# A routed two-expert FFN behind a conditional FFN: first eight sequences in pieces of two, first weight loads ahead of their rows, last piece ranked ahead of the tiles

## What is computed

```python
# 1. conditional FFN: one set of 32 output columns depends on the sequence's index
h = gelu(x @ fc1_w.T + fc1_b)                      # (32, 128, 512)
shared = h @ fc2_w.T + fc2_b                       # 96 columns
expert_x = einsum('bnh,bph->bnp', h, experts_w[indices]) + experts_b[indices]   # 32 columns
y = concatenate([shared, expert_x], -1)            # (32, 128, 128)
# 2. mixture of 8 experts, the top 2 of each token
scores = y @ router_w.T                            # (4096, 8)
top_v, top_i = top_k(scores, 2); routing_w = softmax(top_v)
out = sum over e of (gelu(y @ w1[e].T) @ w2[e].T) * (weight of e for the token)
return x + out
```

## Time and profile before

| | us |
|---|---|
| median of 3 runs | 244.78 |
| lowest and highest of the 3 | 243.59, 251.19 |
| the profiled execution's own time | 242.82 |
| its span (first to last instruction) | 241.1 |
| PE busy | 212.0 (88%) |
| POOL busy | 165.4 (69%) |
| DVE busy | 149.9 (62%) |
| ACT busy | 125.8 (52%) |

### The profile page before, as it was taken

The page is one execution under the profiler, slowest core; times in us unless marked ns, Lnnn a source line. Parts: engine busy times, 40 slices in busy tenths (PEclk is TensorE's granted clock), DMA queues, the critical chain, the costliest instruction groups (busy, mean ns, idle before and its releaser), DMA issues.

```text
span 241.1 us, 3554 instructions
## 1 busy us (share of the span) xinstructions
PE 212.0 (88%) x1107; PEld 168.3 (70%) x1107; DVE 149.9 (62%) x458; ACT 125.8 (52%) x178; POOL 165.4 (69%) x172
## 2 busy tenths in 40 slices
PE   7999999999996269989999999999999999998200
PEld 2768678668766248868888888888888888887100
DVE  3454275366756057869999999986666652213593
ACT  2566745744753026856677666666777623241000
POOL 6306527777777777587878778877887777776710
PEclk9999999999999555999999999999999999999955
DMA  6665546563711695099948966666699918414968
GB/s 171 195 208 169 132 160 198 134 197 123 230 59 45 210 372 234 25 367 366 357 165 284 384 254 238 235 224 230 236 329 371 360 58 263 184 50 137 361 228 325
DMA packets 25860, 53.45 MB, mean 222 GB/s; under 512 B 4936, under 2 KB 11344, under 8 KB 23794
## 3 DMA queue, kind: packets, MB, share of 16 engines
q1 hardware_dynamic: 19648, 42.55, 51.6%
q0 software_dynamic: 4544, 8.54, 10.2%
q10 hardware_dynamic: 1650, 2.16, 2.5%
HBM read 24.34 MB, written 13.02 MB: 155 GB/s over the span
## 4 chain that ended last, share of the span: by engine, by line
POOL 44%; issue 23%; PE 13%; DVE 8%; DMA 7%; ACT 2%; SPq 1%; POOLq 0%; ACTq 0%; DVEq 0%
POOL results L442 28%; POOL slots L435 16%; PE hp L852 4%; PE dd L863 3%; DMA w<-ffn 3%; DMA results<-rows,back_row 2%; PE hp L908 2%; DVE z L832 2%; DVE z L830 2%; PE tr L877 1%; DMA slots<-y_rows,slot 1%; DMA cexp_bias<-in_cexp_b 1%; ACT hs_raw L501 1%; PE misc L841 0%; DVE ffn L725 0%
## 5 line engine op out<-in xcount | busy, mean ns | idle before, releaser
L442 POOL DMA_INDIRECT results<-rows,back_row x78 | 93.0, 1193 | 24.8 <-issue 23.5
L435 POOL DMA_INDIRECT slots<-y_rows,slot x64 | 66.6, 1041 | 37.5 <-DVE slot L632 19.2
L908 PE MATMUL hp<-xs,w 128*128 128x512 f32 x192 | 52.7, 413 | 2.1 <-DMA w<-ffn 2.1
L501 ACT ACTIVATE hs_raw<-hp 128x1024 f32<-128x1024 f32 x32 | 32.8, 1026 | 33.2 <-PE hp L908 33.2
L908 PEld LDWEIGHTS hp<-xs,w 128*128 128x128 f32 x192 | 38.2, 200 | 11.2 <-issue 2.5
L739 DVE TENSOR_TENSOR hs<-hs_raw,hs 128x1024 fp32r<-128x1024 f32 x32 | 39.0, 1219 | 2.8 <-ACT hs L509 2.4
L509 ACT ACTIVATE hs<-hs_raw 128x1024 fp32r<-128x1024 f32 x32 | 33.9, 1061 | 0.5
L467 ACT ACTIVATE hs_raw<-hp,fc_bias 128x512 f32<-128x512 f32 (+1 forms) x36 | 22.8, 640 | 20.3 <-PE hp L852 20.3
L863 PE MATMUL dd<-cond,hs_raw 128*128 128x128 f32 x256 | 32.3, 278 | 0.0
L863 PEld LDWEIGHTS dd<-cond,hs_raw 128*128 128x128 f32 x256 | 30.0, 192 | 0.8 <-issue 0.8
L852 PE MATMUL hp<-xs_raw,fc 128*128 128x512 f32 (+1 forms) x72 | 29.6, 555 | 0.0
(11 more groups left out here) (142 smaller groups left out, 263.6 us busy)
## 6 DMA issues: line engine op xcount, KB each, us to landing
w<-ffn SPq DMA_DIRECT2D x16, 1024.0 KB, 5.5
picked<-slots SPq DMA_DIRECT2D x16, 264.0 KB, 2.8
ffn_raw<-in_wT SPq DMA_DIRECT2D x8, 512.0 KB, 4.7
z<-results SPq DMA_DIRECT2D x8, 512.0 KB, 7.2
narrow_w<-in_wT SPq DMA_DIRECT2D x7, 512.0 KB, 7.5
cond<-in_cexpT SPq DMA_DIRECT2D x32, 64.0 KB, 2.0
x_rows<-in_x SPq DMA_DIRECT2D x1, 2048.0 KB, 10.4
out<-z ACTq DMA_DIRECT2D x8, 256.0 KB, 2.9
```

Source lines behind the costliest of these rows:

```text
L435: pool.indirect_dma_start(out=slots, out_offset=bass.IndirectOffsetOnAxis(ap=slot[:, p, n:n + 1], axis=0), in_=y_rows[:, p % YB, k, r, :], ...
L442: pool.indirect_dma_start(out=results, out_offset=bass.IndirectOffsetOnAxis(ap=back_row[:, t, r:r + 1], axis=0), in_=rows[:, t % RB, r, :] ...
L501: act.activation(hs_raw[:, (NP + t) % 2, 1, g, :], hp[:, g, :], ACT.Gelu).then_inc(c_gelu, 1)
L908: mm = pe.matmul(hp[:, g, n * TILE:(n + 1) * TILE], w[:, t % WB, 0, part, f * P:(f + 1) * P], xs[:, (NP + t) % XB, v, :], start=m == 0, st ...
```

## The change

The first eight sequences are cut into four pieces of two in place of two of two and one of four, so there are ten pieces and `LAST` = 9; `LIST_PIECE` still names the pieces that end at the same sequences. The eight experts are loaded in pieces 0 to 5 (`RAW`) and split two at a time in pieces 4 to 7 (`SPLIT`). `spread_bias(0)` moves behind `up(0)`, `spread_bias(1)` behind `down(1, ...)`, and both use other PSUM banks. SP reads the first list and loads the weights of tiles 0 to 2 before it waits for the scatters of their rows. The last piece's `score` and `rank` on PE, `y_second` and `lean` on ACT, and `choose`, `mark` and `place_pairs` on DVE move ahead of most of the work of tiles 0 to 2. `tile_done` leaves ACT: DVE counts tile t - 3 in `rows_of(t)`, which waited for that landing already, and POOL counts the last three, the first of these before the last tile's scatters.

```diff
@@ -35,14 +35,14 @@
...
-PIECES = (2, 2) + (4,) * (CHUNKS - 1)
+PIECES = (2, 2, 2, 2) + (4,) * (CHUNKS - 2)
 NP = len(PIECES)
...
-LIST_PIECE = (5, 7, LAST)
+LIST_PIECE = (LAST - 3, LAST - 1, LAST)
 LIST_WIDE = (3, 4, 9)
@@ -59,6 +59,11 @@
...
+RAW = ((0,), (1,), (2,), (3,), (4, 5), (6, 7)) + ((),) * (NP - 6)
+SPLIT = ((),) * 4 + ((0, 1), (2, 3), (4, 5), (6, 7)) + ((),) * (NP - 8)
 def blocks(t):
@@ -71,6 +76,11 @@
...
     return 2 * t + g + 1 if t < WIDE else WIDE + t + 1
+def run_after(c):
+    return FIRST.index((c + 1) * RPT)
@@ -210,10 +220,12 @@
...
         misc = ps("misc", [P, TILE])
-        dx = dd[:, 1, :, :].rearrange("p r d -> p (r d)")
-        results_of = (dd[:, 0, :, :].rearrange("p r d -> p (r d)"), misc[:, :])
-        bias_of = (misc[:, :], tr[:, :, :].rearrange("p r d -> p (r d)"))
+        banks = [dd[:, n, :, :].rearrange("p r d -> p (r d)") for n in range(2)]
+        dx = banks[NP % 2]
+        results_of = (banks[LAST % 2], misc[:, :])
+        bias_of = (misc[:, :], banks[0])
@@ -305,8 +317,8 @@
...
                     load_x(p + XB)
-                if p < EXP:
-                    load_expert(p)
+                for e in RAW[p]:
+                    load_expert(e)
                 if p + 2 < NP:
@@ -347,15 +359,19 @@
...
                 sp.wait_ge(s_list, n + 1)
+                sp.sem_inc(s_go, 1)
+                if n == 0:
+                    listed(0, LIST_WIDE[0])
+                    sp.wait_ge(s_wlo, EXP)
+                    for t in range(LIST_WIDE[0]):
+                        load_weights(t)
                 landed(LIST_PIECE[n - 1] + 1 if n else 0, LIST_PIECE[n] + 1)
-                sp.sem_inc(s_go, 1)
                 for t in range(LIST_START[n], LIST_START[n + 1]):
-                    if (t - LIST_START[n]) % 4 == 0:
+                    if n and (t - LIST_START[n]) % 4 == 0:
                         listed(t, min(t + 4, LIST_START[n + 1]))
                     pick(t)
-                    if t == 0:
-                        sp.wait_ge(s_wlo, EXP)
-                    load_weights(t)
+                    if n:
+                        load_weights(t)
                     if t == 4:
@@ -436,13 +452,22 @@
...
+            def tile_done(t):
+                pool.wait_ge(s_zout[t % RB], 16 * scattered(t))
+                pool.sem_inc(s_done, 1)
             for t in range(TILES):
                 pool.wait_ge(c_rows, t + 1)
+                if t == TILES - 1:
+                    tile_done(TILES - RB)
                 for r in range(blocks(t)):
...
                         bounds_check=TOPK * TOKENS - 1, oob_is_err=False).then_inc(s_zout[t % RB], 16)
+            for t in range(TILES - RB + 1, TILES):
+                tile_done(t)
@@ -509,34 +534,31 @@
...
-            def tile_done(t):
-                act.wait_ge(s_zout[t % RB], 16 * scattered(t))
-                act.sem_inc(s_done, 1)
             act.wait_ge(s_fc1b, 16)
-            bias_out(0)
             for p in range(NP):
...
                 if p == 0:
-                    bias_out(1)
+                    bias_out(0)
                 if p:
...
                     y_second(p - 1)
-                if 1 <= p <= EXP:
-                    expert_high(p - 1)
+                for e in SPLIT[p]:
+                    expert_high(e)
                 if p:
                     lean(p - 1)
+                if p == 1:
+                    bias_out(1)
...
             y_turned(LAST)
+            y_second(LAST)
+            lean(LAST)
             tile_gelu(0, 0)
...
             tile_high(0, 0)
-            y_second(LAST)
             tile_gelu(0, 1)
             tile_high(0, 1)
-            lean(LAST)
             for t in range(1, TILES):
@@ -548,10 +570,6 @@
...
                     narrow_gelu(t)
-                if t >= 5:
-                    tile_done(t - 5)
-            for t in range(TILES - 5, TILES):
-                tile_done(t)
             for c in range(CHUNKS):
@@ -577,8 +595,9 @@
...
                     dve.wait_ge(s_spread[p - YB], 16 * TOPK * PIECES[p - YB])
+                if p < 3:
+                    dve.wait_ge(a_bias, 1 + p // 2)
                 if p == 0:
-                    dve.wait_ge(a_bias, 2)
                     dve.wait_ge(s_sharedin, 16)
@@ -712,8 +731,9 @@
...
                 n = c1 - c0
+                runs = slice(run_after(c0), run_after(c1 - 1) + 1, run_after(c0 + 1) - run_after(c0))
                 link(dve.tensor_tensor(
-                    needed[:, c0:c1, :, :], run[:, c0 + 2:c1 + 2, :].unsqueeze(2).to_broadcast((P, n, TILES, EXP)),
+                    needed[:, c0:c1, :, :], run[:, runs, :].unsqueeze(2).to_broadcast((P, n, TILES, EXP)),
                     where_all[:, :].unsqueeze(1).unsqueeze(3).to_broadcast((P, n, TILES, EXP)), ALU.is_gt))
@@ -748,9 +768,19 @@
...
                     dve.wait_ge(s_zout[t % RB], 16 * scattered(t - RB))
+                    dve.sem_inc(s_done, 1)
                 n = blocks(t)
...
                                   rows_in(t)[:, :, P + 1:P + 2].to_broadcast((P, n, P)), ALU.mult).then_inc(c_rows, 1)
+            def merge(c):
+                if c == 0:
+                    dve.wait_ge(s_xrows, 16)
+                dve.wait_ge(s_z[c], 16)
+                dve.tensor_tensor(z[:, c, 0, :], z[:, c, 0, :], z[:, c, 1, :], ALU.add).then_inc(s_sum, 1)
+                dve.wait_ge(s_sum, c + 1)
+                dve.tensor_tensor(z[:, c, 0, :], z[:, c, 0, :], x_rows[:, c, :], ALU.add)\
+                   .then_inc(s_fin, 1)
@@ -782,21 +812,22 @@
...
                     mark(p - 1)
-                    expert_low(p - 1)
+                for e in SPLIT[p]:
+                    expert_low(e)
...
             place_pairs(LAST - 1)
-            early_counts(1)
-            picked_low(1)
-            tile_low(0, 0)
             choose(LAST)
             mark(LAST)
+            place_pairs(LAST)
+            dve.tensor_copy(end_i[:, :], run[:, NP, :]).then_inc(s_end, 1)
+            picked_low(1)
+            early_counts(1)
+            tile_low(0, 0)
             early_list(1)
...
             picked_low(2)
-            place_pairs(LAST)
-            dve.tensor_copy(end_i[:, :], run[:, NP, :]).then_inc(s_end, 1)
             tile_low(1, 0)
@@ -824,13 +855,8 @@
...
-            dve.wait_ge(s_xrows, 16)
             for c in range(CHUNKS):
-                dve.wait_ge(s_z[c], 16)
-                dve.tensor_tensor(z[:, c, 0, :], z[:, c, 0, :], z[:, c, 1, :], ALU.add).then_inc(s_sum, 1)
-                dve.wait_ge(s_sum, c + 1)
-                dve.tensor_tensor(z[:, c, 0, :], z[:, c, 0, :], x_rows[:, c, :], ALU.add)\
-                   .then_inc(s_fin, 1)
+                merge(c)
@@ -955,39 +981,43 @@
...
             keep_clock(9)
-            spread_bias(0)
             for p in range(NP):
...
                 if p == 0:
-                    spread_bias(1)
+                    spread_bias(0)
                     pe.wait_ge(s_fc2, 32)
...
                     pe.wait_ge(s_const, CONSTS + 2)
-                    pe.wait_ge(a_bias, 2)
                 if p:
                     turn_y(p - 1)
+                if p == 2:
+                    pe.wait_ge(a_bias, 2)
                 down(p, 0, 1)
...
                 down(p, 1, PIECES[p])
+                if p == 1:
+                    spread_bias(1)
                 if p:
+                    if p == 1:
+                        pe.wait_ge(a_bias, 1)
                     rank(p - 1)
...
             turn_y(LAST)
+            score(LAST)
             tile_up(0, 0)
+            rank(LAST)
             turn_in(1)
-            score(LAST)
             tile_up(0, 1)
...
             turn_in(2)
-            rank(LAST)
             tile_down(0, 0)
...
             tile_down(0, 1)
```

## The result

The changed kernel takes 250.43 us (median of 4 runs, 248.91 to 250.69); the kernel before, on the same chip, 247.99 (4 runs, 243.59 to 251.55). The ratio is 1.024, 95% interval 1.016 to 1.032; two of the four executions of the kernel before (251.19 and 251.55) ran in a slower state of the chip and are left out of it. So the change is slower, clear of noise, but whether by more than 2% is open; I had forecast 242.4. Measured again later beside its parts it was 1.013 (1.009 to 1.017). The profiled executions are 250.69 (span 249.0) against 242.82 (span 241.1), so between these two 7.9 us are to be found.

A forecast was written before the change was run, and what follows sets the result against it. POOL was taken to bound the first stage, PE from tile 3 on, with the end a third place. Span 241.1 - 0.3 - 1.5 = 239.3, own time 241.0, plus 1.4: 242.4 us; range 239.5 to 245.8.

The forecast's parts named there:

- POOL's wait for tile 20 in front of tile 22's scatters is free: End, on POOL: counting tile 20 there costs 0, since no load of `z` waits for tiles 20 to 22.
- The gain at the end, 1.5 us: Last merges and stores: `z` loads leave 1.9 later, but stores follow their merges directly; 1.5 us gained, between 0.8 and 2.2.
- The first stage: Pieces and slot scatters: slots of sequences 8 to 11 come 0.9 us sooner; `turn_in(3)` nets 0.3 us earlier.
- the 2.9 I took: POOL's scatters before tile 3: total delay from DVE's splits and `tile_low`s, 2.9 us against 2.3 before; ends 0.4 and 5.
- the register loads that I had counted as saved: Ahead of `pick(0)`: some 1.1 us of register loads gone, helping `turn_in(0)` start at about 80.5 instead of 82.77.
- The rival of the falling clock: PE's wait before tile 3 halves its clock afterwards, costing 2.5 to 4.7 us; own time 243.5 to 245.7; chance 0.25.
- the 1.4 us that the forecast and the lower end have: Added to own time to reach the median of timed runs, which lay 1.96 above the profiled one, the lowest 0.77.
- the lower end: Range's bottom, 239.5 us: splits hold POOL's scatters less, own time 238.7, plus 1.4, less 0.6; that rival's chance 0.14.

The follow-up runs named there:

- The run with one wait: Kernel before, plus a POOL wait at its very end for the landing of the last tile's scatter: 247.11 us beside 246.15, ratio 1.0077.
- the warming run: Kernel before, plus twelve of PE's warming matmuls (`keep_clock(12)`) between the last piece and `turn_in(0)`: ratio 1.000 (0.996 to 1.005).
- the quiet runs: Runs without PE halts, beside the kernel before at 245.59 us: changed kernel 1.013; with landings counted on ACT 0.992; also with the last piece ranked late 0.988.
- ACT's counting: Changed kernel with all scatter landings counted by ACT again, as in the kernel before: 278.58 us beside 267.91; later, without PE halts, 243.23 us, ratio 0.992.
- the run that paces PE: Kernel before, with PE waiting ahead of each piece from the fourth on until the piece two before has its slots: ratio 1.006 (1.003 to 1.009).

## Why the prediction was wrong

**The step that failed: "POOL's wait for tile 20 in front of tile 22's scatters is free".** I asked only whether a load of `z` waits for these counts. None does. But POOL waits twice more behind the scatters, and behind that stands the drain that ends its program: a row of the kernel before, 227.6 to 239.1, that I had not read, as it is under no line of POOL's code. It had 1.8 us to spare before SP's end. The run with one wait moved its start by 6.6 us and put its end 2.0 behind SP; in the change its start moved by 12.1, of which 1.8 is PE's lateness, and its end came 4.3 behind. This is shown, by itself (1.0077) and together with the moved count (5.0 us of 248.24).

**The gain at the end, 1.5 us, had the wrong sign.** The loads did leave after `rows_of(20)`, as forecast, 1.8 later by PE's end. I then took 1.5 us a load as if alone. From the first load's issue to SP's drain it is 244.5 - 223.1 = 21.4 us, before 240.9 - 219.4 = 21.5; and 20.7 to 22.4 in all 20 traces, whichever engine counts and whether the stores go one by one (over some 13 us) or in a row (over 4.5). Loads of 4 MB and stores of 2 MB move in that time; with stores among them the last `z` landed 13.6 us after its issue, where 9.7 had been the worst. So stores that start early buy little (20.7 to 21.4 us in the five traces that have them, 21.2 to 22.4 in the others), and a late first load is paid nearly in full: SP's drain stands 17.2 to 17.9 us behind PE's last transposes in those five, 15.8 to 17.0 in the others. That the 21.4 us are set by the volume is argued from these spans; no run changed the volume.

**The first stage was right in its order and too small in its gain.** `up(2)` 15.58 (15.2), `up(5)` 33.76 (33.2), the slots of sequences 8 to 11 at 45.24 (44.75); the scatters on which tile 3 rests were held for 1.8 us and not for the 2.9 I took, so the scatter at 97.15 came 0.9 earlier and not 0.3. `turn_in(0)` came at 82.31, not 80.5: its scatter ended at 76.2 and its landing took 3.2, so the register loads that I had counted as saved probably lay beside that landing. As forecast this moved nothing further on.

**The rival of the falling clock came true in the first execution.** Its gap was 2.19 us, its price 1.6 (2.5 forecast). The clock had fallen behind the first gap too, 5.03 us long (mean 0.56 from 84 to 92), so it fell behind both gaps and not behind one of the two. In the later execution of the same kernel the gap before tile 3 was 0.78 and the clock did not fall there; the warming run, with 3.39, shows it again. "TensorE: Matmul & The Clock Gate", section "HAM oscillation — how this bites in real kernels", of the Trainium skill has a DMA wait, if it is long enough, throttle PE and the next work start cold. The traces show this behind 2.19, 2.39 and 3.39 us, and a clock that stays up behind 0.78, 0.84, 1.16, 1.51 and (in the run with one wait) 1.66. So it is not a fixed cost of the change but one that comes and goes with a microsecond in POOL's stream; it and the 0.6 us by which tile 7's rows came late (SP waited 4.8 us for the landing of the filler rows, and `turn_in(7)` came 7.07 after `turn_in(6)`, 6.44 in the kernel before) make up 2.2 of the 2.4 us by which the way from `turn_in(3)` to the last transposes grew (226.6 - 103.5 against 224.8 - 104.2).

**Against the sum:** forecast -0.3 and -1.5. Found in the first profile: -0.65 at `turn_in(3)`, +1.6 clock, +0.6 fillers, +6.1 tail. In the quiet runs, where the clock does not fall at tile 3 and the fillers cost 0.1 to 0.9 (6.50, 7.04 and 7.38 for the same step): +5.0 for the counting, -2 to -3 for all the rest. The range was also narrower than its own rival: the clock's 243.5 to 245.7 leaves out the 1.4 us that the forecast and the lower end have, and with it would reach 247.1. The measured 250.43 lies beyond that too.

**Open.** What makes PE halt in the midst of work in twelve runs and not in the other six (one chip showed both), and why the early ranking then costs 9 and 8 us by the medians of two comparisons, is not settled: the run that paces PE was made for it and met no halt. The verdicts on the parts from those runs should not be carried over; the quiet runs reversed one of them (ACT's counting, 1.02 to 1.04, then 0.992). The pieces of two and the early weights were not timed alone in quiet runs.

## What to carry to other kernels

An engine's program does not end with its last instruction: look at the closing rows of each engine and at how much room they have before the end of the span. A wait placed last on the engine with the longest drain is paid for once that room is used up; let an engine whose drain is short (here ACT, 0.15 us, or PE, 0.49) do the final counting.

In a tail of loads and stores like this one, ask first when its first load leaves: what follows took 20.7 to 22.4 us here, however the stores were ordered. And time a part of a change beside the kernel before on a chip on which that kernel runs at its usual time, before giving the part a price.

## What the hardware did that I had not expected

POOL's closing drain takes 9.05 us behind its last wait; where it does not wait its record is 11.5 to 12.1 us long and ends 9.0 to 9.1 us behind that of its last scatter. Those of DVE, PE, ACT and SP take 0.73, 0.49, 0.15 and 0.007 (PE's took 0.008 in the run in which PE waits last). What waits for PE can be released up to 6 us behind PE's own records, in several stretches of a run (kernel before 267 us instead of 246).
